# A second expert's token list written inside the first expert, a third one in its twelfth step, and filling products behind an attention's last output

## The reference

```
h = weight[x]                                   # 8 x 512 tokens, 256 wide
h = h + attention(layernorm(h))                 # 8 heads of 128, causal
xt = layernorm(h).reshape(4096, 256)
scores = softmax(xt @ Wr, axis=-1)              # 8 experts
G, idx = top_k(scores.T, 1024)                  # each expert takes its 1024 best tokens
X_in = xt[idx]
hid = gelu(X_in @ W1 + b1)                      # 256 -> 1024
X_e = hid @ W2 + b2                             # 1024 -> 256
out = h + scatter_add(G * X_e at idx)
```

## Time and profile before

| | us |
|---|---|
| median of 3 runs | 1184.82 |
| profiled execution | 1191.39 |
| its span | 1189.6 |
| TensorE busy | 1143.3 (96%) |
| VectorE busy | 825.0 (69%) |
| ScalarE busy | 721.2 (61%) |
| GpSimd busy | 821.1 (69%) |
| mean granted clock | 0.996 |

### The profile page before, as it was taken

One profiled execution on the slowest core, in us unless ns is written; L12 is line 12 of the kernel. 1 busy time (PEld: TensorE's weight loads), 2 busy tenths in 40 slices (PEclk: granted clock), 3 DMA queues, 4 the chain that ended last, 5 costly groups with the idle time before them and its releaser, 6 DMA issues. The chain is left out here.

```text
span 1189.6 us, 20415 instructions
## 1 busy us (share of the span) xinstructions
PE 1143.3 (96%) x7120; PEld 997.1 (84%) x7120; DVE 825.0 (69%) x1994; ACT 721.2 (61%) x1537; POOL 821.1 (69%) x921
## 2 busy tenths in 40 slices
PE   7899999999999999999999998779999999999997
PEld 4788888888888888888888885358999999999996
DVE  5998887887887887887888867864455554554433
ACT  4667677686686676676676765315465555555642
POOL 4798897897897898887987854052474484664425
PEclk9999999999999999999999999999999999999999
DMA  5000100100100100200101003322362452523213
GB/s 199 10 10 1 45 28 2 45 28 1 45 28 1 55 18 2 71 2 29 43 2 36 19 1 114 110 69 75 61 139 33 111 127 31 129 51 94 32 23 36
DMA packets 43030, 58.13 MB, mean 49 GB/s; under 512 B 8944, under 2 KB 34992, under 8 KB 42800
## 3 DMA queue, kind: packets, MB, share of 16 engines
q0 software_dynamic: 13824, 21.24, 10.0%
q1 hardware_dynamic: 29104, 35.58, 8.8%
HBM read 35.71 MB, written 16.91 MB: 44 GB/s over the span
## 5 line engine op out<-in xcount | busy, mean ns | idle before, releaser
L1462 DVE TENSOR_TENSOR hT_lo<-hid,hT_hi 128x512 fp32r<-128x512 f32 x124 | 86.2, 695 | 170.7 <-ACT hT_hi L1638 155.6
L312 ACT ACTIVATE prob<-prob,row_min 128x512 f32<-128x512 f32 (+3 forms) x256 | 141.8, 557 | 103.0 <-DVE row_min L539 103.0
L1635 ACT ACTIVATE hid<-up,b_e 128x512 f32<-128x512 f32 x128 | 88.1, 688 | 156.9 <-PE up L1790 137.0
L227 POOL TENSOR_SCALAR prob<-prob,row_inv 128x512 f32<-128x512 f32 (+3 forms) x256 | 134.8, 541 | 12.3 <-DVE row_inv L552 10.3
L1176 POOL DMA_INDIRECT x<-routed_rows,tokens x64 | 81.4, 1272 | 76.7 <-DVE tokens L1456 38.8
L235 POOL TENSOR_TENSOR q_sin<-q_sin,rope_t 128x512 f32<-128x512 f32 x64 | 82.7, 1292 | 73.7 <-ACT q_sin L336 73.7
L444 DVE TENSOR_TENSOR pT_lo<-bank,pT_hi 128x384 fp32r<-128x384 f32 (+1 forms) x192 | 110.2, 594 | 15.4 <-ACT pT_hi L288 14.2
L1187 POOL TENSOR_SCALAR y<-y,gate 128x256 f32<-128x256 f32 x60 | 32.2, 548 | 127.1 <-issue 126.4
L1196 POOL DMA_INDIRECT out<-y,tokens x60 | 98.6, 1643 | 16.2 <-issue 13.9
L799 PE MATMUL bank<-ident,prob 128*128 128x128 f32 x640 | 102.1, 274 | 5.7 <-POOL prob L227 5.0
L288 ACT ACTIVATE pT_hi<-bank 128x384 fp32r<-128x384 f32 (+1 forms) x192 | 96.5, 519 | 13.7 <-PE bank L799 13.3
(11 more groups left out here) (337 smaller groups left out, 3895.3 us busy)
## 6 DMA issues: line engine op xcount, KB each, us to landing
raw<-in_w SPq DMA_DIRECT2D x16, 1024.0 KB
emb_res<-emb SPq DMA_DIRECT2D x8, 512.0 KB, 3.8
out<-h SPq DMA_DIRECT2D x8, 512.0 KB, 2.9
routed_rows<-x SPq DMA_DIRECT2D x8, 512.0 KB, 3.0
x<-in_wq SPq DMA_DIRECT2D x2, 512.0 KB, 6.4
x<-in_wk SPq DMA_DIRECT2D x2, 512.0 KB, 6.4
x<-in_wv SPq DMA_DIRECT2D x2, 512.0 KB, 4.1
x<-in_wo SPq DMA_DIRECT2D x1, 1024.0 KB, 10.1
```

What stands on the lines that cost most here:

```text
L227: nc.gpsimd.tensor_scalar(pr, pr, row_inv[:, h % 2, k:k + 1], 1.0, ALU.mult, ALU.mult).then_inc(s["norm_done"], 1)
L312: nc.scalar.activation(pr, pr, ACT.Exp, bias=row_min[:, h % 2, k:k + 1], scale=-1.0, accum_out=row_sum[:, h % 2, k:k + 1]).then_inc(s["exp ...
L1462: nc.vector.tensor_tensor(out, in_, hi.bitcast(F32), ALU.subtract)\
L1635: nc.scalar.activation(hid[:, t % 2, :], up_ps[t % 2][:], ACT.Gelu, bias=bias)
```

## The change

Four things, all in the engines' programs; nothing of what is computed changes.

1. Ten fillers (`warm(10)`) behind the attention's last products, ahead of the barrier.
2. Fillers before list 0: 20 instead of 16. Behind it: 25 instead of 18, and before each group of `first_turn` 4 instead of 2.
3. List 1 leaves the stretch before the first expert. Inside expert 0, VectorE makes its one-hots at step 0, TensorE sums it behind step 3, VectorE writes it at step 4. GpSimd's gather of expert 1, which waits for it, is in the same place of GpSimd's program.
4. List 2 moves back within expert 0: one-hots at step 11 instead of 0, TensorE's products behind step 13 instead of 4, VectorE's writing at step 14 instead of 5. From expert 1 on all stands as it was.

```diff
@@ build_attention, TensorE
             batches(pe, body)
+            warm(10)
@@ build_middle, VectorE
             dve.wait_ge(s["placed"], 2)
-            one_hots(1)
-            write_list(1, 1)
             for f in range(2):
                 xt_low(0, 0, f)
@@ VectorE, body, behind hT_lo of step t and results()
+                    if e == 0 and t == 0:
+                        one_hots(1)
+                    if e == 0 and t == 4:
+                        write_list(1, 1)
                     if more2:
-                        if t == 0:
+                        if t == (11 if e == 0 else 0):
                             one_hots(e + 2)
-                        if t == 5:
+                        if t == (14 if e == 0 else 5):
                             write_list(e + 2, i)
@@ TensorE, first_turn
                 for c in range(TB):
-                    warm(2)
+                    warm(4)
@@ TensorE, before the first expert
-            warm(16)
+            warm(20)
             pe.wait_ge(s["hot_b0"], 1)
             write_list(0)
-            warm(18)
-            write_list(1)
+            warm(25)
             first_turn()
@@ TensorE, body, behind up and down of step t
-                    if more2 and t == (4 if e == 0 else 2):
+                    if e == 0 and t == 3:
+                        write_list(1)
+                    if more2 and t == (13 if e == 0 else 2):
                         write_list(e + 2)
```

## The result

The changed kernel takes 1188.61 us (median of 7 runs, 1187.11 to 1190.68), the kernel before beside it 1185.11 (7 runs, 1183.53 to 1185.68). The ratio is 1.0032 with a 95% interval of 1.0023 to 1.0042: 3.5 us slower. The forecast was 3.5 us more, 1188.4.

A forecast was written before the change was run, and what follows sets the result against it. TensorE was taken to bound the kernel, never stopping from the second expert on. Terms 0.4 + 1.04 + 2.1 = +3.5 us on 1191.39 profiled give 1194.9, less 6.57: 1188.4 us; 8-in-10 range 1180.5 to 1190.5.

The forecast's parts named there:

- ten products at the barrier, cost: Behind the attention, ten added products end near 722.1, level with SP's store of h: 0, at most 0.2 us.
- their gain (clock): Behind the barrier, the added products gain 0, since the first transposes there already run at full clock.
- fillers and list 1 ahead of expert 0: Before expert 0, fillers rather than gathers now end last, 789.2 against 788.8: +0.4 us.
- a second list inside expert 0: TensorE sums two lists inside expert 0 instead of one, priced from the chain of waits: +1.04 us.
- one-hots in step 11: In expert 0, VectorE's four operations delay e_xT1lo, so TensorE's second transposes wait: +2.1 us, bounds 0 and 4.0.
- The stall: TensorE's wait in step 12 of expert 0 for VectorE's e_xT1lo, behind the moved one-hots: +2.1 us.
- the late gathers: GpSimd's gathers for experts 1 and 2 move later inside expert 0: cost 0, with 6 us to spare.
- the 0.95 us of that rule: At step 6, VectorE's w_1lo could wait for expert 1's gather and delay TensorE's step 8: up to +0.95 us.
- Late signals all gone: Rival, chance 0.22: TensorE's late signals between 785 and 802 and the slow clock behind them go: 7.4 us, 1181.0 us.
- the 6.57 us: Gap of the profiled execution, 1191.39 us, above the median; carried over unchanged to turn 1194.9 profiled into 1188.4.
- The stall lowers the clock: Rival, chance 0.14: TensorE's 2.1 us idle at step 11 brings a half-rate stretch costing 1.7 us: 1190.1 us.
- The stall covered: Rival, chance 0.07: the one-hots are hidden in step 11 as in step 0, leaving 1.4 us of cost: 1186.3 us.

The follow-up runs named there:

- the repeated profile: The kernel before, unchanged, profiled a second time on chip A: 1185.44 us in the profiled execution beside a median of 1185.54.

## Why the prediction was right

Forecast and result agree within 0.2 us. Two of its four terms held, two were off by two or three tenths each, a gain was missing, and the misses cancelled. That the total came out within 0.2 us is luck; that it came out at three to four is not, since the largest term was right by its mechanism.

| term | predicted | measured | where |
|---|---|---|---|
| ten products at the barrier, cost | 0 | 0 | after, store to TensorE 0.83 against 0.82 |
| their gain (clock) | 0 | −0.6 to −0.7, likely | profiles on A and B |
| fillers and list 1 ahead of expert 0 | +0.4 | +0.7 | first list to first product 12.23 against 11.55 |
| a second list inside expert 0 | +1.04 | +1.24 | experts 0 of two kernels, 49.56 and 47.22 |
| one-hots in step 11 | +2.1 | +2.2 | wait 2.02; expert 0 51.79 against 49.56 |
| sum | +3.5 | +3.5 (+4.2 without the likely gain) | |

**The stall** was the largest term, and its mechanism and size were right: VectorE's own dates and the four durations in its way gave 2.1, the wait is 2.02, and moving the one-hots two steps ahead takes it away, with 2.23 us of expert 0.

**Fillers.** The order of the dates was right (fillers last, gathers covered), 0.3 short: from list start to the last transpose's end the prediction has 11.3 us, the trace 11.56, since 0.16 us of the last transpose were left out (a duration of 0.27 of which 0.11 was counted) and the fillers and pairs of transposes together came out 0.1 longer. The four ahead of the first list cost nothing, as predicted: from the first one-hot operation to the list 2.50 us, in the kernel before 2.49. "If the fillers were free" was given as −0.7; without them the run shows −0.5.

**The list.** The prediction had two rows, 1.04 on the chain and 1.24 from expert 6, and took the first as nearer. The second was right: taking a whole piece out and reading the length of the stage prices what goes with it, the record of the piece does not.

**The ten products.** The step that put their gain at nothing read a clock of 1.00 in the one profile it had. Others of the same kernel had 0.50 in the same place.

**GpSimd.** As predicted, nobody waits for the late gathers, and with more to spare than the 6 us of the prediction: expert 2's gather starts at 841.53 and not at 847, the scatter-add behind it ends at 863.5 and not at 872, and VectorE writes that buffer again at 875.2. VectorE's low weights and the gathers beside them in after:

```profile
810.78 0.94 POOL L1177 DMA_INDIRECT x<-routed_rows,tokens  x1 [0.30 <-issue]
811.43 2.28 DVE L1463 TENSOR_TENSOR w_1lo<-raw,w_1hi 128x2048 fp32r<-128x2048 f32 x1
812.03 2.50 POOL L1177 DMA_INDIRECT x<-routed_rows,tokens  x1 [0.30 <-issue]
```

Beside the earlier trace rows: VectorE's 2.28 us are the undisturbed time; GpSimd's gather takes 2.50 where the ones around it take 0.95. By the rule that was weighed from the Trainium skill (SBUF — State Buffer, "Who interferes with whom") whichever of the two comes second waits. Where that is GpSimd the trace agrees: the gather issued at 812.03, beside a w_1lo begun at 811.43, ends at 814.53, 0.8 us behind its end at 813.71. Where it is VectorE the trace does not: w_1lo starts at 811.43 beside the gather of 810.78 to 811.72, right as VectorE's hT_lo ends, and neither is longer for it (in the kernel before such a gather, at 824.32, took 1.09). So the 0.95 us of that rule were not paid.

**The rivals.** *Late signals all gone* (0.22) happened in after's profile and did not bring its time, since the timed runs of before beside it had none to lose, as far as the repeated profile shows: the kernel before without them is at 1185.4. The step that decided it was to carry the 6.57 us over unchanged. That was right for the median and wrong for the profiled run (1194.9 forecast, 1188.19 measured): the 6.57 us were no constant of the recording but the late signals and slow clock of the profile that was read, as the near equality with 7.4 had hinted. The other reading, by which the 6.57 us were such a constant, is not borne out: of the profiles taken later 1185.44 stands beside a median of 1185.54, 1188.19 beside 1188.61, 1192.62 beside 1192.13. That is no test of what the Trainium skill says (Runtime: NRT & Kernel Launch, "The ~15µs preamble/postamble breakdown"), a profile's total some 6.2 us above the time reported without it: every timed run on record has a granted clock and a span beside it, the span 1.8 to 1.9 us shorter than the time, just as the profiled ones have, and no time here is known to be one without a profile. On chip C the rival's mechanism probably decided the sign: the change seems to save part of what late signals and clock take there, and the kernel is 2.6 us faster in spite of the 4.1 us of cost. That is argued from the changed kernels' profiles; the kernel before has none that is known to be of this chip. The prediction's range, 1180.5 to 1190.5, does not hold the time on that chip, nor does it hold the one of the kernel before. *The stall lowers the clock* (0.14): not on A or B or in after, but in all three profiles on C that have the stall, 1.5 us each, close to the 1.7 it was priced at. *The stall covered* (0.07) fell.

**Open.** What makes TensorE's signals late. They stand beside rows of gathers in every trace that has them, on C also later than expert 0, and no run took the gathers away. What the kernel before spends 9.6 us more on when it runs on chip C. And 2.0 of the 3.7 us between the kernels with and without the added fillers there.

## What to carry to other kernels

An operation moved within an engine's order is priced by the dates of what stands behind it, and the same four microseconds of one-hots cost 2.2 us in step 11 of the first expert, 1.1 in its step 0 and nothing that shows in its step 9, while in step 0 of experts 1 to 5 TensorE waits for nothing: look for the step that has no hand-over behind it before giving up a move. Where a profiled execution is well above the median, find what in it is of that execution, or of its chip, alone before adding anything to its time: here one more profile of the unchanged kernel would have said so. Fillers cost time as soon as what they wait out ends sooner (here 1.2 us), and a gain of a quarter of a per cent should be seen on more than one chip before it is believed.

## What the runs showed of the hardware

- One kernel, one program: 1184.9 to 1185.5 us on two chips and 1194.7 to 1194.8 on a third, in 33 runs there and 56 on the others, without overlap. The changed kernel differs by 3.5 us between them, so the sign of the comparison does too (1.0032 and 0.998).
- Instructions of ScalarE or VectorE that start 1.9 to 3.7 us behind the end of TensorE's products that they read, with their own engine idle, beside or right behind rows of indirect gathers, in the first profile of before and in all four on chip C, and in none of the eight on A and B nor in after.
- After some 2 us of idle time of TensorE (2.2 at the barrier, 2.0 in step 12) the granted clock falls to 0.50 for about 3.4 us in some profiles and not in others with the same idle time. Behind the barrier it fell in three of six. Behind step 12 it fell in three of three profiles on C, and in none of three elsewhere (A, B and after). Each fall costs 1.4 to 1.6 us.
- A two-input VectorE operation over 128x2048 is not slowed by a gather beside it (2.28 us), and a gather issued while it runs goes from 0.95 to 1.90 or 2.50 us: it ends 0.8 us behind the VectorE operation both times.
